# Sixteen-head attention blocks on one core: scores turned by sequence in two 64-row tiles, the values' products moved to another bank, the phases written out

## What is computed

```
L0_SELF   pre-norm, causal                     L0_CROSS  pre-norm, keys from ctx, then MLP (pre-norm, GELU)
L1_CROSS  RMS-norm, rotary q and k, keys from ctx
L2_SELF   causal and key mask, norm after      L2_CROSS  key mask, norm after, then MLP, norm after
L3_SELF   pre-norm                             L3_CROSS  pre-norm, keys from ctx, then MLP (pre-norm, GELU)

each:  s = q k^T / sqrt(8) (masked);  p = softmax(s);  x = x + (p v) W_o + b_o
```

## Time and profile before

| | |
|---|---|
| median of 3 runs | 2357.57 us (2356.8 to 2361.8) |
| profiled execution | 2359.6 us, of which span 2357.8 us |
| PE, PEld busy | 2216.8 us (94%), 1837.2 us (78%) |
| DVE, ACT, POOL busy | 1839.3 (78%), 1682.8 (71%), 1385.4 us (59%) |
| chain that ended last | PE 46%, POOL 23%, issue 21% |
| granted clock of PE | full in all but a few slices; mean 0.985 |

### The profile page before, as it was taken

The page is one execution under the profiler, slowest core; times in us unless marked ns, Lnnn a source line. Parts: engine busy times, 40 slices in busy tenths (PEclk is TensorE's granted clock), DMA queues, the critical chain, the costliest instruction groups (busy, mean ns, idle before and its releaser), DMA issues.

```text
span 2357.8 us, 100357 instructions
## 1 busy us (share of the span) xinstructions
PE 2216.8 (94%) x37613; PEld 1837.2 (78%) x37613; DVE 1839.3 (78%) x4653; ACT 1682.8 (71%) x3278; POOL 1385.4 (59%) x3557
## 2 busy tenths in 40 slices
PE   2799999999999999999998999999999999999997
PEld 2688878788877887878887877777888878787876
DVE  3588887788777888878776888777877888887864
ACT  0477757788876775878886776677878877577876
POOL 3355446886554443888554544588756544388843
PEclk6899999999999999999999999999999999999999
DMA  6355455444444455444554545544455444544432
GB/s 149 100 138 131 125 135 131 115 121 126 126 124 114 127 129 137 125 114 116 131 132 109 133 126 132 141 114 122 120 129 130 121 117 115 137 126 115 119 100 59
DMA packets 310611, 289.39 MB, mean 123 GB/s; under 512 B 50080, under 2 KB 251552, under 8 KB 310112
## 3 DMA queue, kind: packets, MB, share of 16 engines
q1 hardware_dynamic: 305120, 279.80, 46.5%
q10 hardware_dynamic: 4128, 1.65, 0.4%
q0 software_dynamic: 864, 1.28, 0.3%
HBM read 130.51 MB, written 34.60 MB: 70 GB/s over the span
## 4 chain that ended last, share of the span: by engine, by line
PE 46%; POOL 23%; issue 21%; DVE 3%; DMA 2%; SPq 2%; ACT 2%; POOLq 1%; DVEq 0%; ACTq 0%
PE ps_scores_t L844 9%; PE ps_scores L807 6%; PE ps_out L832 5%; PE ps_turn L892 4%; PE ps_wide L914 4%; POOL x_bias L676 4%; POOL pre_rstd L618 2%; PE ps_wide L873 2%; PE ps_wide L872 2%; POOL post_rstd L618 2%; PE ps_turn L897 2%; PE ps_wide L882 2%; PE ps_out L903 2%; POOL post_normed L657 2%; PE ps_wide L911 2%
## 5 line engine op out<-in xcount | busy, mean ns | idle before, releaser
L1138 DVE TENSOR_REDUCE row_max<-ps_scores 128x16 f32<-128x1024 f32 x448 | 548.5, 1224 | 336.8 <-PE ps_scores L807 171.3
L746 ACT ACTIVATE probs<-ps_scores_t 128x512 f32<-128x512 f32 x896 | 535.1, 597 | 130.5 <-PE ps_scores_t L844 88.7
L1144 DVE TENSOR_TENSOR shifted<-ps_scores,row_max 128x512 f32<-128x512 f32 x896 | 577.4, 686 | 15.4
L844 PE MATMUL ps_scores_t<-ident,shifted 128*128 128x128 f32 x3584 | 567.6, 281 | 7.2 <-ACT probs L746 5.5
L844 PEld LDWEIGHTS ps_scores_t<-ident,shifted 128*128 128x128 f32 x3584 | 395.0, 142 | 54.3 <-issue 7.1
L736 ACT COPY pv_sb<-ps_out 128x256 f32<-128x256 f32 x448 | 167.7, 374 | 248.8 <-PE ps_out L832 247.4
L807 PE MATMUL ps_scores<-k_slots,qk_rows 32*64 32x256 f32 x7168 | 311.9, 401 | 26.1 <-issue 14.2
L832 PEld LDWEIGHTS ps_out<-probs,v_ones 128*32 128x32 f32 x14336 | 222.6, 110 | 140.8 <-issue 140.2
L832 PE MATMUL ps_out<-probs,v_ones 128*32 128x64 f32 x14336 | 294.6, 223 | 2.6 <-issue 1.3
L741 ACT ACT_TABLE_LOAD x190 | 243.8, 1283 | 3.4
L746 ACT ACT_TABLE_LOAD x189 | 242.5, 1283 | 3.4
(11 more groups left out here) (169 smaller groups left out, 4595.7 us busy)
## 6 DMA issues: line engine op xcount, KB each, us to landing
v_ones<-v_rows SPq DMA_DIRECT2D x1792, 64.0 KB
k_slots<-k_dram SPq DMA_DIRECT2D x448, 256.0 KB
k_dram<-qk_rows SPq DMA_DIRECT2D x448, 64.0 KB
x_in<-in_x SPq DMA_DIRECT2D x64, 64.0 KB, 1.9
ctx_in<-in_ctx SPq DMA_DIRECT2D x64, 64.0 KB, 1.9
out<-x SPq DMA_DIRECT2D x64, 64.0 KB, 1.6
k_dram<-zeros SPq DMA_DIRECT2D x4, 256.0 KB, 6.4
w<-in_L_xattn_W SPq DMA_DIRECT2D x2, 256.0 KB, 7.2
```

The costliest lines, as they stand in the source:

```text
L746: nc.scalar.activation(probs[:, u, :, :], ps_scores_t[:, :] .rearrange("p (h t) -> p h t", h=4), ACT.Exp, scale=SCALE).then_inc(probs_read ...
L844: ins = nc.tensor.transpose(ps_scores_t[:, h * P:(h + 1) * P], shifted[:, j % 2, u, h * P:(h + 1) * P], ident[:, :])
L1138: v.tensor_reduce(row_max[:, :].rearrange("p (g n) -> p g n", n=SLOTS), ps_scores[:, :, 0:256].rearrange("p g (n k) -> p g n k", k=LEN), A ...
L1144: v.tensor_tensor(shifted[:, j % 2, u, :].rearrange("p (g n k) -> p g n k", n=SLOTS, k=LEN), ps_scores[:, 2 * u:2 * u + 2, 0:256].rearrang ...
```

## The change

**Turning the scores.** Eight full turns of 128x128 become sixteen turns of 64 rows by 128 columns. Each takes the scores of one sequence (partitions 0 to 63 or 64 to 127) for two heads, and the two sequences write two different banks, `ps_scores_t[:, 0]` and `[:, 1]`. All sixteen are issued together; there is no second half later in the phase. ACT's two exponentials are now by sequence and stand one behind the other.

**Values.** The products of probabilities and v move from `ps_out`, which is gone, to the first half of `ps_turn`. They therefore wait for ACT's `copy_turned` of the phase before, and whoever writes `ps_turn` next (down, project) waits for `copy_pv` first (`pv_taken`). The turned result (`pv_t`) goes to bank 0 of `ps_scores_t`, after the first exponential has read it. `turned` gets two buffers.

**Order on PE.** `turns` comes ahead of the MLP's up; L1_CROSS's v product (`rope_v`) comes behind `turns` and writes bank 1 of `ps_scores_t`.

**Order on ACT and DVE.** ACT copies `turned` ahead of the GELU. DVE makes the residual sum between the two shifts, unless the phase has a down; the norms' statistics of the sums come after the second shift.

**Mask.** For L2_CROSS, whose key mask is the same for all queries, eight bf16 instructions (one row taken by `quad_first`) replace sixteen.

**Phases.** All phases are written out; there is no loop.

```diff
-        probs = sb("probs", [P, HALVES, 4, P])
+        probs = sb("probs", [P, SEQS_OF_PAIR, HEADS // 2, LEN])
-        turned = sb("turned", [P, 4, P])
+        turned = sb("turned", [P, 2, 4, P])
-        ps_scores_t = banks("ps_scores_t")
-        ps_out = banks("ps_out")
+        ps_scores_t = banks("ps_scores_t", SEQS_OF_PAIR)
...
-            for j in range(-STATS, FIRST):
+        PHASES = range(-STATS, UNITS + LAG * STREAMS + DOWN + 2)
+        def rounds(phase):
+            for j in PHASES:
                 phase(0, j)
-            with eng.Fori(0, ROUNDS - 1) as r:
-                for j in BODY:
-                    phase(r, j)
-            for j in LAST:
-                phase(ROUNDS - 1, j)
...
+                    if layer == L2_CROSS:
+                        for g in range(QUADS):
+                            of_g = slice(32 * g, 32 * g + 32)
+                            for b in range(2):
+                                ins = nc.tensor.matmul(ps_scores[64 * b:64 * b + 64, g, 0:256], quad_first[of_g, :],
...
                 def values(r, j):
-                    pe.wait_ge(attn_ready.sem, attn_ready.at(r, j - 1))
...
-                                ins = nc.tensor.matmul(ps_out[32 * h:32 * h + 32,
+                                ins = nc.tensor.matmul(ps_turn[32 * h:32 * h + 32,
...
-                def transposes(r, j, u):
-                    pe.wait_ge(shifted_ready.sem, shifted_ready.at(r, j, u + 1))
-                    if u:
-                        pe.wait_ge(probs_ready.sem, probs_ready.at(r, j, 1))
-                    for h in range(4):
-                        ins = nc.tensor.transpose(ps_scores_t[:, h * P:(h + 1) * P],
-                                                  shifted[:, j % 2, u, h * P:(h + 1) * P], ident[:, :])
+                def transposes(r, j):
+                    if exists(r, j - VALUES):
+                        pe.wait_ge(attn_ready.sem, attn_ready.at(r, j - VALUES))
+                    if exists(r, j + QKV) and layer_of(j + QKV) == L1_CROSS:
+                        pe.wait_ge(rope_v_ready.sem, rope_v_ready.at(r, j + QKV))
+                    pe.wait_ge(shifted_ready.sem, shifted_ready.at(r, j))
+                    for h in range(HEADS // 2):
+                        for b in range(SEQS_OF_PAIR):
+                            ins = nc.tensor.transpose(ps_scores_t[:, b, h * LEN:(h + 1) * LEN],
+                                                      shifted[64 * b:64 * b + 64, j % 2, h // 4, h % 4 * P:h % 4 * P + P],
+                                                      ident[64 * b:64 * b + 64, 64 * b:64 * b + 64])
...
                 def phase(r, j):
                     if exists(r, j):
                         scores(r, j)
+                    turned_free(r, j)
+                    if not turned_parts(r, j - 1):
+                        residuals_read(r, j - 1)
                     if exists(r, j - VALUES):
                         values(r, j - VALUES)
                     if exists(r, j - 1):
-                        transposes(r, j - 1, 0)
-                    turned_free(r, j)
-                    if not turned_parts(r, j - 1):
-                        residuals_read(r, j - 1)
+                        transposes(r, j - 1)
+                    if exists(r, j - VALUES):
+                        pv_taken(r, j - VALUES)
...
```

More of the change, by code:

```diff
@@ L49 @@
 HALVES = 2
+SEQS_OF_PAIR = 2
 HCH = HID // P
@@ L570, in _, with phase @@
                 sp.wait_ge(rows_cleared, 16 * RING)
-                def phase(r, j, this, following):
+                def phase(r, j):
                     if exists(r, j + QKV - 1):
@@ L577, in phase @@
                     i = j - FIRST
-                    if following is not None and i >= 0 and layer_of(i) == L0_SELF and in_program(i):
-                        load_next(r, i, following)
+                    if exists(r, i) and layer_of(i) == L0_SELF and round_of(i) + 1 < ROUNDS:
+                        load_next(r, i, round_of(i) + 1)
                     i = j - DOWN - 1
                     if exists(r, i) and layer_of(i) == L3_CROSS:
[L582 to L590, removed]
-                    phase(ROUNDS - 1, j, ROUNDS - 1, None)
+                        store(r, i, round_of(i))
+                rounds(phase)
                 for s in range(STREAMS):
@@ L971, in phase @@
                         pv_t(r, j - VALUES)
-                    if exists(r, j - 1):
-                        transposes(r, j - 1, 1)
+                    if turned_parts(r, j):
+                        turns(r, j)
+                    if exists(r, j + QKV) and layer_of(j + QKV) == L1_CROSS:
+                        rope_v(r, j + QKV)
                     if has_mlp(r, j - UP):
                         mlp_up(r, j - UP)
-                    if turned_parts(r, j):
-                        turns(r, j)
-                rounds(pe, phase)
+                rounds(phase)
             @block.vector
@@ L1190, in phase @@
                         maxima(r, j)
+                    late = has_mlp(r, j - DOWN)
+                    if exists(r, j):
                         shift(r, j, 0)
-                        shift(r, j, 1)
-                    if has_mlp(r, j - DOWN):
+                        if late:
+                            shift(r, j, 1)
+                    if late:
                         mlp_residual(r, j - DOWN)
@@ L1196, in phase @@
                         residual(r, j - OUT)
+                    if exists(r, j) and not late:
+                        shift(r, j, 1)
+                    if has_mlp(r, j - DOWN):
+                        mlp_post_norm_begin(r, j - DOWN)
+                    if exists(r, j - OUT):
+                        post_norm_begin(r, j - OUT)
                     if rope:
```

105 lines of the change are left out of this document (57 added, 48 removed).

## The result

The changed kernel takes 2329.05 us (median of 4 runs, 2326.22 to 2331.38), the kernel before 2357.19 on the same chip: ratio 0.9875, 95% interval 0.9862 to 0.9888. That is 28 us for a forecast of 126, and 4 us above the range.

What follows compares the result with a forecast made beforehand. PE was taken as the main bound, POOL in 61.6 us of a 508.2 us round. 13.7 + 4.5 + 7 = 25.2 us a round made 106, plus 20 for the loop: 2357.6 - 126 = 2232 us, range 2175 to 2325.

Steps and rivals of the forecast that it cites:

- What bounds the kernel: Second round, 508.2 us: PE alone paces 284.6, PE and DVE are busy in 121.4 rotary, POOL paces 61.6.
- own sign, two stretches unchanged: Sign to look for in the trace: POOL's stretches of 61.6 us stay unchanged in each round.
- Part 1, the turns: Score turns on PE: pairs at 0.06 us, group 0.72 for 0.93; gain 0.21 a down phase, 0.35 an up phase.
- Part 2, the pair of phases: MLP phases: up 4.74 for 4.92, down 4.46 for 4.67; 4.8% of 284.6 us, 13.7 us a round.
- q, k copy at 2.93, v at 3.20: ACT's copies in an up phase, counted from `scores`: done at 3.47, up may start at 3.53, PE waits 0.16.
- rival 3: ACT becomes the limit, as PE reads its results at two earlier points: 0.25 us lost a pair, 2270 us; chance 0.20.
- Part 3, DVE's order: Residual sum one shift earlier: 4.5 us a round in nine phases without MLP, 7 us in the rotary stretches.
- Part 4, the loop: Writing out the phases removes 20.1 us at the loop's two turns, with no price seen for more code.
- Head and tail: Start and end of the run, with chains of one unit: 0 gain.

Runs made afterwards that it cites:

- experiment 7: Kernel before with its phases written out, POOL's product with `post_g` left out of L2's three norms: 2318.07 us, 0.984 of the kernel before.
- experiment 8: Changed kernel with POOL's product with `post_g` left out of L2's three norms: 2281.12 us, 0.9669 of the kernel before.
- experiment 10: Changed kernel with the 128x128 part of L3_SELF's norm as one DVE instruction, one phase later, replacing two on POOL: 2297.95 us, 0.9747 of the kernel before.
- experiment 2: Changed kernel with eight full 128x128 turns replacing the sixteen of 64 rows, same place and banks: 2363.11 us, 1.0031 of the kernel before.
- Experiment 3: Changed kernel with the sixteen turns unpaired, eight of one sequence and then eight of the other: 2410.88 us, 1.0227 of the kernel before.
- experiment 9: Changed kernel with DVE's order of before, both shifts and then the residual sum, in every phase: 2361.72 us, 1.002 of the kernel before.
- experiment 1: Kernel before with its phases written out in place of the loop, nothing else changed: 2340.57 us, 0.9934 of the kernel before.

## Why the prediction was wrong

**What bounds the kernel** is the step that failed first, and it weighs most. The prediction gave POOL two stretches, 61.6 us, from busy times of windows cut where PE's pace changed, and called the rest of these phases PE's alone. But POOL waits for only 6.7 us in the 159.4 of phases 184 to 214, never longer than 2.0. In the phases around the two stretches PE ran at its own pace only because POOL was ahead by then, and what PE gains there it pays back at the next wait for POOL. Forecast for these phases -4.7 us a round, measured +1.9; experiments 7, 8 and 10 show POOL as the cause. A part of it is the half clock after the longer stalls: the stretch grew by 4.0, 1.8, 2.7 and 1.8 us in the four rounds, and in the first and third the clock fell twice, behind the waits of 2.7 and 3.1 us, in the others once. The prediction's own sign, two stretches unchanged, did not hold either: phases 192 to 197 went from 31.9 to 31.4 us, and 208 to 213, with the stall of 3.1 in them, from 29.7 to 33.2.

**Part 1, the turns**: right in the mechanism and in the size. 0.74 for 0.72, with the pairs, the change of tiling and the load that nothing hides each about as forecast; the form is worth 37 us of the run (experiment 2). The Trainium skill's page "TensorEngine Tiling (Array Packing)", section "Key Properties", says that different tiles can load and multiply in parallel. The trace agrees: the two turns of a pair start 0.003 to 0.004 us apart, a pair every 0.062 us. Experiment 3 adds that here only neighbours in the program did. The rule of the Trainium skill's page "TensorE: Matmul & The Clock Gate", section "LDWEIGHTS", that the prediction weighed, columns over 1.2, gives 0.107 us for one load of 128 columns. The trace differs for these turns: their loads step at 0.062 us.

**Part 2, the pair of phases**: the down phase was right (4.48 for 4.46), the up phase was not (4.97 for 4.74). The step that failed is ACT's "q, k copy at 2.93, v at 3.20": 2.93 is when PE has issued all of qkv and goes on to `pv_t` (measured 2.96). The last matmul of qkv ends 0.17 after that, and the copy starts at 3.16, so copies and up come 0.23 later (3.76 for 3.53), and PE's wait is 0.36 for 0.16. The rows had shown it: the copy at 1127.43 starts 0.20 after PE has gone on to `pv_t`, 0.22 ahead of the turns at 1127.45. On top, the scores' change of tiling, 0.09, went behind the up (0.99 for 0.89); the sum had that. The prediction saw in this way a wait of 0.14 behind the second half of the turns, and not that the way hid the other 0.44 of them.

In the phases behind a turn of the context there is a second loss, read from the trace alone. ACT copies `ctx_t` ahead of `turned`; the values, which wait for `turned` only since the change, come 0.19 late, and the up phase is 5.14, more than before's 4.92. (Over the whole run PE's loading for the values waits for `turned` 75.9 us, 197 times, not all of it PE's loss.) That is rival 3's mechanism, at three quarters of its size and only in these pairs. Together, the 27 phases that PE paces (182, 183 and 215 to 239) gained 2.2% for a forecast 4.8%.

**Part 3, DVE's order**: in the rotary stretches (phases 144 to 155 and 160 to 171) the mechanism was right and the size half: -3.8 us in the second round for -7, 14.2 over the four. With the old order it is all given back (experiment 9: 485.4 us over the four rounds, before 485.2, changed 471.0). In the nine phases without MLP (172 to 180) -0.7 for -4.5 in the second round, and nothing over the four (159.2 us before, 160.7 now). There the step named no next limit behind DVE, and there was one. In phases 167 to 181 PE waited 4.2 us for the residual sum and 1.8 for k_slots before; now 1.1 and 8.2; with the old order on DVE again (experiment 9) 6.4 and 1.3. The one wait takes the place of the other: a slower phase had hidden k's way out to DRAM and back.

**Part 4, the loop**: 20 us at its two turns, right. Written out, the kernel keeps 15 of them; 4.6 us more in POOL's stretches stand against them (experiment 1), which the prediction did not have.

**Head and tail**: 0 forecast, +5.3 us in the first 8 and last 7 intervals between two starts of `scores`. No run tells why.

For the 96 phases of the second round (477.5 us before): 144 to 166 -3.9, 167 to 181 -1.0, 184 to 214 +1.9, and the 27 that PE paces -2.9. That is -5.9 us where the forecast had some -24 (25.2 less 4.8% of the 30.7 us that are not in them). Of the 18 us that are missing, 6.6 are in POOL's stretch, 3.4 in the phases that PE paces, and the other 8 in phases 144 to 181, rotary and without MLP. The like phases of the first and third rounds gave 2.2 and 2.4 us, and with the loop's 20 it is 34 of the span.

## What to carry over

Before a gain of the busiest engine is spread over a stretch, look for another engine that hardly waits there. Here its idle time told it (6.7 us of waits in 159.4, none longer than half a phase) and its share did not (86% busy, PE 97%). An engine can be the limit over a stretch in which the busy one waits only three times. To be sure, take work from it and see whether the stretch gets shorter. When work is taken out from between two steps, ask whether it stood in a round trip of another engine: take the trip's length from the end of the last matmul, not from its issue. Two orders that are changed together have to be priced together: DVE's order looked like 8 to 20 us from the two traces and was worth 34 beside PE's new one. And when a wait goes, ask which one stood behind it.

## What the hardware showed that was not expected

- The two row tiles worked at once all through the group only when neighbouring instructions were on different tiles: 0.64 us paired, 0.945 unpaired (three of eight beside each other), 0.93 as eight full turns. Unpaired, the form gains nothing.
- A full 128x128 turn takes 0.109 us from start to start in a row of four and in a row of eight. The 0.49 and 0.93 of the groups behind `values` come from their first turn, which takes 0.165. An unpaired 64-row turn takes 0.062.
- After 3.1 us of idling PE's granted clock was 0.50 for 3.0 us, in which it had twelve matmuls; the 2.8 us behind them had 0.99 again. In the four rounds the 3 us behind this wait had 0.73, 0.51, 0.50 and 0.50. After the waits of 2.7 us it was 0.50 in two of four rounds and 1.00 in the others; after those of 1.6 to 2.0 in the kernel before it was 1.00 each time.
- SP's issues fill 57.7 of 62.5 us in phases 167 to 180, one in 0.64 us, and taking two of six away changed the time by an unclear 0.16%: a queue that is nearly full by its busy time need not be the limit.
